# One selection product and a reciprocal of 512 columns in the second attention of a two-layer kernel

## The chip, the cores and the metric

The kernel runs on one core of a Trainium2 chip. The metric is the time of one execution on the device, in microseconds (us), lower being better. The engines are TensorE (PE in the profile; its weight loads are PEld), VectorE (DVE), ScalarE (ACT), GpSimd (POOL) and SyncE (SP, which here only issues transfers).

## The reference, cut to what matters

A batch of 8 sequences of 512 tokens with 256 channels goes through two layers, each an attention and a feed-forward part. The second attention, in which the change lies, has 16 heads of 16 channels, masked scores of 512 queries by 512 keys for each head, and a softmax:

```
scores = jnp.einsum('bhqd,bhkd->bhqk', query, key) / jnp.sqrt(jnp.asarray(D_K, query.dtype))
scores = jnp.where(m == 0, NEG_INF, scores)
probs = jax.nn.softmax(scores, axis=-1)
out = jnp.einsum('bhqk,bhkd->bhqd', probs, value)
out = out.transpose(0, 2, 1, 3).reshape(bs, -1, D_MODEL)
return out @ Wo + bo
```

The kernel divides by the softmax's sums only after the product with the values. The values carry a column of ones, so each head's result has 16 rows of channels and one row with the sum.

## The kernel before, in words

The kernel has three stages one after the other: `first_layer`, `cross_attention` (the second attention) and `experts` (the last feed-forward part). All that is said below is of `cross_attention`.

The 8 sequences are its batches. The 16 heads of a batch are taken in 4 groups of 4 heads, numbered through all batches as g = 0 to 31. A group takes 4 units, one for each 128 keys, so there are 128 units, and some more ahead and behind. Every engine has a program of its own that runs over the same units in order (`UNITS_RUN`), and semaphores tie the programs together. There is no planner: the order within a unit is written out in each engine's loop.

In one unit, for each of 4 heads (k = 0 to 3), TensorE makes the scores of 128 keys by 512 queries (`scores`: a bias product, line 1063, and the product of keys and queries, line 1064), and ScalarE takes their exponential (line 1202). Beside that, for each k, TensorE makes one product of 128 queries by 512 keys for a head of a group that comes 6 units later (`scores_for_maximum`, line 1049), and VectorE takes its masked row maximum (`maximum`, line 1321). These products have two banks, so TensorE waits before the third for VectorE to be through with the first (`wait(pe, s1_used, m - 1)`). Maxima end with unit 121.

After the four k, TensorE does in this order: the early events of bank `ps_m`, the product of the exponentials with the values of the unit before (`values`, line 1076), the query and key/value projections of a later token tile (once in 4 units each; for tiles up to 31), and the late events of bank `ps_m`. The maxima of a group are split in two parts (`split_maxima`, lines 1331 and 1333), turned by TensorE (event rows, line 1099), copied (line 1213) and placed as two more rows of the queries by a transfer (line 1220), for which the first scores of that group wait. Once in a batch, at the start of the batch's ninth unit, SyncE issues 24 transfers that spread the split queries and keys of the next batch (`spread_part`, line 872), after the rows of the group then due have landed.

The sums of group g are treated so:

- ScalarE copies the group's result to OT, 128 rows by 512 queries, head j in rows 32j to 32j+16 (`copy_o`, line 1208). The sum of head j is row 32j+16.
- Late in unit 4g+5 TensorE takes the sums out (event sums, line 1103): four products with OT as weights and the 4 columns of `pick`, so that the 512 queries lie on the partitions, 4 sums for each.
- At the end of unit 4g+5 VectorE inverts these 16 columns (`invert_sums`, line 1339) and copies each value 32 times (line 1341).
- Late in unit 4g+6 TensorE turns the result back with 4 transposes (event spread, line 1106), and VectorE multiplies OT by it (`divide`, line 1346).
- At the start of unit 4g+6 VectorE does the next `split_maxima` and then two maxima.

Of the kernel before, what the change touches and what calls it, by code (L numbers as in the profile page):

```python
# [11 lines left out]
P = 128  # L12
# [3 lines left out]
TPB = SEQ // P  # L16
# [713 lines left out]
def bank_m_events(unit):  # L730

    early, late = [], []
    if group_at(unit - 5) is not None:
        late.append(("sums", group_at(unit - 5)))
    if group_at(unit - 6) is not None:
        late.append(("spread", group_at(unit - 6)))
    if group_at(unit + 2) is not None:
        early.append(("rows", group_at(unit + 2)))
    b, u = divmod(unit, UNITS)
    if 1 <= b <= BATCH and u in (3, 4):  # L740
        early.append(("output", TPB * (b - 1) + 2 * (u - 3)))
        late.append(("output", TPB * (b - 1) + 2 * (u - 3) + 1))
    return early, late


def cross_attention(nc, ctxT, mask, maskT, L1, X, tg, ident_f, stats, mu_rs, kept, ahead):
# [3 lines left out]
    with ExitStack() as ctx:  # L750
# [14 lines left out]
        ident_b = sb("ident_b", [P, P], BF16)  # L765
        pick = sb("pick", [P, 4])
        v_scale, v_shift = sb("v_scale", [P, GROUPS]), sb("v_shift", [P, GROUPS])
# [14 lines left out]
        OT = sb("OT", [P, SEQ])  # L782
        r4 = sb("r4", [P, TPB, 4])
        r32 = sb("r32", [P, TPB, 4, 32])
        OTn = sb("OTn", [P, GROUPS, SEQ])
# [38 lines left out]
        for unit in UNITS_RUN:  # L824
            for events in bank_m_events(unit):
                for e in events:
                    m_use[e], m_before[e], last = len(m_use), last, e
                    if e[0] in ("spread", "output"):
                        m_freed[e] = len(m_freed) + 2
# [91 lines left out]
        def _(pool):  # L921
# [5 lines left out]
            def constants():  # L927
                pool.memset(ident_b[:, :], 0.0).then_inc(consts, 1)
                pool.memset(pick[:, :], 0.0).then_inc(consts, 1)
                pool.memset(v_scale[:, :], 0.0).then_inc(consts, 1)  # L930
                pool.memset(v_shift[:, :], 0.0).then_inc(consts, 1)
                pool.memset(wo[:, :, :], 0.0).then_inc(consts, 1)
                for p in range(3):
                    pool.memset(V[p][:, :, :, DH:VW], 1.0).then_inc(consts, 1)
                pool.wait_ge(consts, 4)
                pool.affine_select(out=ident_b[:, :], in_=ident_b[:, :], compare_op=ALU.not_equal, fill=1.0,
                                   base=0, pattern=[[-1, P]], channel_multiplier=1).then_inc(consts, 1)

                pool.affine_select(out=pick[:, :], in_=pick[:, :], compare_op=ALU.not_equal, fill=1.0,
                                   base=-DH, pattern=[[-32, 4]], channel_multiplier=1).then_inc(consts, 1)  # L940

# [67 lines left out]
        def _(pe):  # L1009
# [70 lines left out]
            def bank_m(event):  # L1080
                what, n = event
                if what == "rows":
                    pe.wait_ge(max_split, n + 1)
                elif what == "sums":
                    pe.wait_ge(o_sb, n + 1)
                elif what == "spread":
                    pe.wait_ge(inverted, n + 1)
                before = m_before[event]
                if before is None:
                    pe.wait_ge(m_free, 1)  # L1090
                elif before[0] == "rows":
                    pe.wait_ge(rows_sb, before[1] + 1)
                elif before[0] == "sums":
                    pe.wait_ge(inverted, before[1] + 1)
                else:
                    pe.wait_ge(m_free, m_freed[before])
# [4 lines left out]
                elif what == "sums":  # L1101
                    for q in range(TPB):
                        mm = pe.matmul(ps_m[:, 4 * q:4 * q + 4], OT[:, q * P:(q + 1) * P], pick[:, :], start=True, stop=True)
                elif what == "spread":
                    for q in range(TPB):
                        mm = pe.transpose(ps_m[:, q * P:(q + 1) * P], r32[:, q, :, :].rearrange("p j c -> p (j c)"), ident_f[:, :])
                else:
# [43 lines left out]
        def _(act):  # L1151
# [52 lines left out]
            def copy_o(g):  # L1204
                act.wait_ge(pv_done, TPB * (g + 1))
                if g:
                    act.wait_ge(m_free, m_freed["spread", g - 1])
                act.activation(OT[:, :], ps_o, ACT.Copy).then_inc(o_sb, 1)
# [43 lines left out]
        def _(dve):  # L1252
# [82 lines left out]

            def invert_sums(g):
                use = m_use["sums", g]
                dve.wait_ge(m_ready, use + 1)
                steps.done(dve.reciprocal(r4[:, :, :].rearrange("p q h -> p (q h)"), ps_m[:, 0:4 * TPB]))
                steps.wait()  # L1340
                dve.tensor_copy(r32[:, :, :, :], r4[:, :, :].unsqueeze(3).broadcast_to([P, TPB, 4, 32])).then_inc(inverted, 1)

            def divide(g):
                use = m_use["spread", g]
                dve.wait_ge(m_ready, use + 1)
                dve.tensor_tensor(OTn[:, g % GROUPS, :], OT[:, :], ps_m, ALU.mult).then_inc(m_free, 1)
# [13 lines left out]
            for unit in UNITS_RUN:  # L1360
# [19 lines left out]
                for what, n in late:  # L1380
                    if what == "sums":
                        invert_sums(n)
                    elif what == "spread":
                        divide(n)
# [615 lines left out]
```

## Time and profile before

| What | Before |
|---|---|
| median of 3 runs | 2315.28 us (2314.14 to 2317.16) |
| the profiled execution, its own time | 2316.27 us |
| its span, first to last instruction | 2314.5 us |
| TensorE busy, share of the span | 85% |
| VectorE busy, share of the span | 68% |
| mean granted TensorE clock | 0.914 |
| second attention, from about | 560 us to 1451 us |

Busy time of TensorE is the time in which at least one product runs, and a product's end is modelled, so two neighbours overlap in the records; the pitch from one start to the next tells what a product costs. A releaser is the instruction whose signal ended a wait.

### The profile page before, as it was taken

The page shows a single profiled execution, that of the slowest core. Times are in us where ns is not written, and L with a number is a line of the kernel's source. Part 1 is how long each engine was busy: PE and PEld are TensorE (multiplying, and loading weights), DVE is VectorE, ACT ScalarE, POOL GpSimd, SP SyncE. Part 2 cuts the span into 40 slices and gives each one's busy share as a digit, 9 for nine tenths or more (in the row PEclk, how much of TensorE's full clock was granted, in tenths as well). Part 3 has the DMA queues.
Part 4 walks back from the last instruction along what each step waited for, and adds up shares of the span by engine and source line. Part 5 has one row for each costly group of instructions (what it writes and reads, how often), then busy time and mean ns, then how long its engine had stood idle before and what let it go on. Part 6 is the DMA issues. An engine that isn't in the chain of part 4 may idle for free. (4 is left out here: it accounts for less than half of the span.)

```text
span 2314.5 us, 35806 instructions
## 1 busy us (share of the span) xinstructions
PE 1966.5 (85%) x12086; PEld 1392.0 (60%) x12086; DVE 1576.7 (68%) x3208; ACT 1059.8 (46%) x2039; POOL 919.2 (40%) x671
## 2 busy tenths in 40 slices
PE   5889888977598988989898989700999999999998
PEld 3566666664233433434343434600999999999998
DVE  7999999984565655656565753630777777777775
ACT  2233434433255554545555544210566566556554
POOL 6988888863433332323332200155222222222222
PEclk9899999988699999999999998555999999999999
DMA  7100000101624425151515310242566666666662
GB/s 286 43 10 8 10 10 10 35 1 34 109 74 67 84 53 102 32 105 33 97 60 78 76 21 1 73 173 91 189 222 227 211 225 222 224 224 216 228 216 68
DMA packets 146909, 245.79 MB, mean 106 GB/s; under 512 B 14235, under 2 KB 92143, under 8 KB 146802
## 3 DMA queue, kind: packets, MB, share of 16 engines
q1 hardware_dynamic: 135660, 218.93, 34.1%
q0 software_dynamic: 10624, 25.26, 2.9%
q8 instruction: 56, 0.92, 0.2%
q14 instruction: 51, 0.42, 0.1%
q10 hardware_dynamic: 518, 0.27, 0.0%
HBM read 201.96 MB, written 45.76 MB: 107 GB/s over the span
## 5 line engine op out<-in xcount | busy, mean ns | idle before, releaser
L1321 DVE CUSTOM_DVE_ANT_0 x_dump<-x_ps,x_bias_q 128x512 bf16<-128x512 f32 x512 | 353.3, 690 | 200.6 <-PE x_ps L1049 188.1
L1202 ACT ACTIVATE x_PT<-x_ps 128x512 f32<-128x512 f32 x512 | 290.1, 601 | 292.2 <-PE x_ps L1064 289.3
L1063 PE MATMUL x_ps<-x_bias_k,x_ident_b 128*128 128x512 bf16 x512 | 201.1, 393 | 66.5 <-DMA x_QS<-x_rows 66.4
L1852 ACT ACTIVATE e_silu<-m_ps 128x256 f32<-128x256 f32 x312 | 118.6, 380 | 231.9 <-PE m_ps L1789 231.9
L1756 POOL DMA_INDIRECT out_dram<-e_y,e_label x78 | 78.9, 1012 | 365.4 <-DVE e_y L1908 353.6
L1049 PE MATMUL x_ps<-x_KS,x_QS 96*128 96x512 bf16 x512 | 203.6, 399 | 12.0 <-DVE x_mx L1321 11.5
L1064 PE MATMUL x_ps<-x_QS,x_KS 98*128 98x512 bf16 x512 | 200.2, 391 | 0.0
L1891 DVE TENSOR_TENSOR e_gated<-e_silu,m_ps 128x256 f32<-128x256 f32 x312 | 120.7, 417 | 102.5 <-ACT e_silu L1852 98.0
L1789 PE MATMUL m_ps<-e_x_lo,m_hi 128*128 128x256 f32 x640 | 181.1, 283 | 1.5 <-DVE e_x_lo L1876 1.5
L1789 PE MATMUL m_ps<-e_x_hi,m_lo 128*128 128x256 f32 x640 | 181.0, 283 | 0.0
L1789 PE MATMUL m_ps<-e_x_hi,m_hi 128*128 128x256 f32 x640 | 180.7, 282 | 0.0
L1789 PE MATMUL m_ps<-e_x_hi,e_hi 128*128 128x256 f32 x608 | 171.1, 281 | 0.0
L1789 PE MATMUL m_ps<-e_x_lo,e_hi 128*128 128x256 f32 x608 | 171.1, 281 | 0.0
L1789 PE MATMUL m_ps<-e_x_hi,e_lo 128*128 128x256 f32 x608 | 171.1, 281 | 0.0
L1458 DVE TENSOR_TENSOR m_lo<-m_raw,m_hi 128x2048 fp32r<-128x2048 f32 x60 | 137.2, 2287 | 38.2 <-ACT m_hi L1454 38.2
L282 POOL TENSOR_TENSOR a_pool_pv<-a_e,a_v 128x2304 f32<-128x2304 f32 x32 | 162.6, 5080 | 0.0
L1749 POOL DMA_INDIRECT e_y<-out_dram,e_label x78 | 84.6, 1084 | 164.1 <-DMA out_dram<-e_y,e_label 137.7
L1458 DVE TENSOR_TENSOR e_lo<-m_raw,e_hi 128x2048 fp32r<-128x2048 f32 x57 | 130.4, 2287 | 26.3 <-ACT e_hi L1454 26.3
L1076 PE MATMUL x_ps<-x_PT,x_V 128*17 128x512 f32 x1024 | 136.9, 598 | 0.0
L1063 PEld LDWEIGHTS x_ps<-x_bias_k,x_ident_b 128*128 128x128 bf16 x512 | 53.8, 105 | 132.2 <-DMA x_QS<-x_rows 81.9
L1049 PEld LDWEIGHTS x_ps<-x_KS,x_QS 96*128 96x128 bf16 x512 | 50.9, 100 | 124.7 <-DVE x_mx L1321 91.7
L1454 ACT ACTIVATE m_hi<-m_raw 128x2048 fp32r<-128x2048 f32 x60 | 115.0, 1916 | 23.0 <-DMA m_raw<-in_L_ffn_w_dram 23.0
(291 smaller groups left out, 5517.4 us busy)
## 6 DMA issues: line engine op xcount, KB each, us to landing
m_raw<-in_L_ffn_w_dram SPq DMA_DIRECT2D x117, 1024.0 KB, 5.1
parts<-x_part SPq DMA_DIRECT2D x24, 512.0 KB, 3.7
expert_in<-a_blank SPq DMA_DIRECT2D x1, 10062.0 KB, 28.4
e_x<-expert_in SPq DMA_DIRECT2D x39, 258.0 KB, 5.8
x_QS<-parts SPq DMA_DIRECT2D x48, 192.0 KB, 8.8
x_KS<-parts SPq DMA_DIRECT2D x48, 192.0 KB, 12.1
next_mask_k<-in_maskT_dram SPq DMA_DIRECT2D x32, 256.0 KB, 2.7
next_mask_q<-in_mask_dram SPq DMA_DIRECT2D x29, 256.0 KB, 2.8
```

The lines of the kernel that those rows point to most:

```text
L282: pool.tensor_tensor(heads(pool_pv[:, :], PV_POOL), probabilities(e_[t % 2][:, PV_OWN * H:], PV_POOL), values(v_sb[t % 3][:, :], PV_POOL), ...
L1049: pe.matmul(ps_max[m % 2], QS[b % 2][0:HROWS, h, q * P:(q + 1) * P], KS[b % 2][0:HROWS, h, :], start=True, stop=True).then_inc(s1_ps, 1)
L1063: pe.matmul(ps_st[e % 3], ident_b[:, :], bias_k[b % 2][:, kc, :], start=True, stop=False)
L1064: pe.matmul(ps_st[e % 3], KS[b % 2][:, h, kc * P:(kc + 1) * P], QS[b % 2][:, h, :], start=False, stop=True).then_inc(st_ready, 1)
L1076: mm = pe.matmul(ps_o[32 * j:32 * j + VW, :], V[b % 3][:, kc, 4 * g + j, :], PT[unit % 2][:, j, :], start=(kc == 0), stop=(kc == TPB - 1))
L1202: act.activation(PT[unit % 2][:, k, :], ps_st[e % 3], ACT.Exp, scale=DH ** -0.5).then_inc(exp_done, 1)
L1321: dve.tensor_tensor_reduce(out=dump[:, :], in0=ps_max[m % 2], in1=bias_q[b % 2][:, q, :], scale=1.0, scalar=NEG, op0=ALU.add, op1=ALU.max, ...
L1454: act.activation(w_hi[p][n][:, :, :], raw[n][:, :, :], ACT.Copy).then_inc(hi_done[n], 1)
L1458: eng.tensor_tensor(w_lo[p][n][:, :, :], raw[n][:, :, :], w_hi[p][n][:, :, :].bitcast(F32), ALU.subtract)\
L1789: mm = pe.matmul(out, left[a], right[b], start=first and n == 0, stop=last and n == 2)
L1852: act.activation(silu[f % 2][:, :], ps_h[f % 4][:, 0:BLK], ACT.Silu).then_inc(silu_done, 1)
L1891: dve.tensor_tensor(gated[k % 2][:, n, :], silu[n][:, :], ps_h[f % 4][:, BLK:2 * BLK], ALU.mult)\
```

## The change

The transposes of the event spread go, and so do the tiles `r4` and `r32` and the function `invert_sums`. `pick` becomes 128 columns wide: column 32j+c has its one in row 32j+16, for each c of 0 to 31. It is now the weights, and OT streams: one product of 128x128 weights with 512 columns puts each head's sum in all 32 rows of that head. VectorE takes the reciprocal of the whole 128x512 bank in place, in `divide`, and multiplies OT by it right after; both are late in unit 4g+5. The wait of the next user of `ps_m`, and of the next `copy_o`, is for `divide` in that unit.

```diff
-    if group_at(unit - 6) is not None:
-        late.append(("spread", group_at(unit - 6)))
...
-        pick = sb("pick", [P, 4])
+        pick = sb("pick", [P, 4, 32])
...
-        r4 = sb("r4", [P, TPB, 4])
-        r32 = sb("r32", [P, TPB, 4, 32])
...
-                    if e[0] in ("spread", "output"):
+                    if e[0] in ("sums", "output"):
...
-                pool.memset(pick[:, :], 0.0).then_inc(consts, 1)
+                pool.memset(pick[:, :, :], 0.0).then_inc(consts, 1)
...
-                pool.affine_select(out=pick[:, :], in_=pick[:, :], compare_op=ALU.not_equal, fill=1.0,
-                                   base=-DH, pattern=[[-32, 4]], channel_multiplier=1).then_inc(consts, 1)
+                pool.affine_select(out=pick[:, :, :], in_=pick[:, :, :], compare_op=ALU.not_equal, fill=1.0,
+                                   base=-DH, pattern=[[-32, 4], [0, 32]], channel_multiplier=1).then_inc(consts, 1)
...
-                elif what == "spread":
-                    pe.wait_ge(inverted, n + 1)
...
-                elif before[0] == "sums":
-                    pe.wait_ge(inverted, before[1] + 1)
...
-                    for q in range(TPB):
-                        mm = pe.matmul(ps_m[:, 4 * q:4 * q + 4], OT[:, q * P:(q + 1) * P], pick[:, :], start=True, stop=True)
-                elif what == "spread":
-                    for q in range(TPB):
-                        mm = pe.transpose(ps_m[:, q * P:(q + 1) * P], r32[:, q, :, :].rearrange("p j c -> p (j c)"), ident_f[:, :])
+                    mm = pe.matmul(ps_m, pick[:, :, :].rearrange("p j c -> p (j c)"), OT[:, :], start=True, stop=True)
...
-                    act.wait_ge(m_free, m_freed["spread", g - 1])
+                    act.wait_ge(m_free, m_freed["sums", g - 1])
...
-            def invert_sums(g):
-                use = m_use["sums", g]
-                dve.wait_ge(m_ready, use + 1)
-                steps.done(dve.reciprocal(r4[:, :, :].rearrange("p q h -> p (q h)"), ps_m[:, 0:4 * TPB]))
-                steps.wait()
-                dve.tensor_copy(r32[:, :, :, :], r4[:, :, :].unsqueeze(3).broadcast_to([P, TPB, 4, 32])).then_inc(inverted, 1)
-
             def divide(g):
-                use = m_use["spread", g]
-                dve.wait_ge(m_ready, use + 1)
+                dve.wait_ge(m_ready, m_use["sums", g] + 1)
+                dve.reciprocal(ps_m, ps_m).then_inc(inverted, 1)
+                dve.wait_ge(inverted, g + 1)
                 dve.tensor_tensor(OTn[:, g % GROUPS, :], OT[:, :], ps_m, ALU.mult).then_inc(m_free, 1)
...
                     if what == "sums":
-                        invert_sums(n)
-                    elif what == "spread":
                         divide(n)
```

## Rows read from the trace of the kernel before

**Rows 1.** Windows, 1050 to 1100 us: time, busy (count) per engine, PEclk, DMA.
```profile
1050.00:1100.00 50.00, 49.51 (x259) 22.70 (x257) 32.14 (x103) 26.47 (x55) 15.28 (x16) 1.00 0.12 38
```

**Rows 2.** Waits, 700 to 1400 us: waiter, releaser, total us, times, longest.
```profile
PEld x_ps L1063 <- DMA x_QS<-x_rows: 77.2, 13, 12.3
PEld x_ps L1049 <- DVE x_mx L1321: 68.3, 190, 0.6
```

**Rows 3.** Timeline, the unit after a group's sums: start, us, engine, instruction, idle before.
```profile
1045.63 1.05 PE L1103 MATMUL x_ps<-x_pick,x_OT 128*128 128x4 f32 x8
...
1046.55 0.38 PE L1063 MATMUL x_ps<-x_bias_k,x_ident_b 128*128 128x512 bf16 x1
...
1047.08 0.25 DVE L1339 RECIPROCAL x_r<-x_ps 128x16 f32<-128x16 f32 x1
...
1047.36 0.43 DVE L1341 COPY x_r<-x_r 128x512 f32<-128x512 f32 x1
...
1048.06 0.69 DVE L1321 CUSTOM_DVE_ANT_0 x_dump<-x_ps,x_bias_q 128x512 bf16<-128x512 f32 x1
...
1048.81 0.10 PEld L1049 LDWEIGHTS x_ps<-x_KS,x_QS 96*128 96x128 bf16 x1 [0.37 <-DVE x_mx L1321]
```

**Rows 4.** Timeline, TensorE's 128x512 f32 products of a key/value tile.
```profile
1039.66 1.96 PE L1015 MATMUL x_ps<-next_wkv,next_cT 128*128 128x512 f32 x4 [0.32 <-ACT x_full L1184]
1041.55 0.39 PE L1017 MATMUL x_ps<-next_bias,x_ones 3*128 3x512 bf16 x1
```

**Rows 5.** Timeline, the end of another unit 4g+6.
```profile
1021.38 0.66 PE L1106 MATMUL x_ps<-ident_f,x_r 128*128 128x128 f32 x4
...
1021.88 0.38 PE L1063 MATMUL x_ps<-x_bias_k,x_ident_b 128*128 128x512 bf16 x1
...
1022.08 0.69 DVE L1346 TENSOR_TENSOR x_OTn<-x_OT,x_ps 128x512 f32<-128x512 f32 x1 [2.06 <-PE x_ps L1106]
```

**Rows 6.** Groups of instructions by form on VectorE: count, busy us, mean ns.
```profile
L1339 DVE RECIPROCAL x_r<-x_ps 128x16 f32<-128x16 f32 x32 | 8.1, 254 | 19.5 <-PE x_ps L1103 19.5
L555 DVE RECIPROCAL a_rden<-a_den 128x16 f32<-128x16 f32 x32 | 7.8, 243 | 0.0
L1647 DVE RECIPROCAL r_share<-r_den 128x32 f32<-128x32 f32 x1 | 0.4, 353 | 0.0
```

**Rows 7.** Timeline, SyncE's and ScalarE's transfers of one batch, and TensorE's wait.
```profile
1002.58 1.26 SPq L872 DMA_DIRECT2D x_QS<-parts  x3
...
1022.51 1.19 ACTq L1220 DMA_DIRECT2D x_QS<-x_rows  x2
...
1033.08 0.61 PE L1063 MATMUL x_ps<-x_bias_k,x_ident_b 128*128 128x512 bf16 x1 [7.38 <-DMA x_QS<-x_rows]
```

**Rows 8.** Windows of 4 us after waits of TensorE; PEclk is the last number but two.
```profile
716.20:720.20 4.00, 4.00 (x13) 2.03 (x14) 0.98 (x3) 1.19 (x2) 1.92 (x1) 0.54 0.24 67
...
1002.60:1006.60 4.00, 4.00 (x13) 2.03 (x14) 1.40 (x4) 1.28 (x3) 0.35 (x1) 0.57 0.39 110
...
1340.60:1344.60 4.00, 4.00 (x10) 1.45 (x11) 1.40 (x4) 1.61 (x3) 1.92 (x1) 0.51 0.02 8
...
1108.50:1112.50 4.00, 4.00 (x24) 1.67 (x24) 2.58 (x7) 3.00 (x8) 1.11 (x1) 1.00 0.43 110
```

**Rows 9.** Timeline of TensorE, two of the short waits for rows.
```profile
1002.58 0.39 PE L1063 MATMUL x_ps<-x_bias_k,x_ident_b 128*128 128x512 bf16 x1 [1.94 <-DMA x_QS<-x_rows]
...
1108.48 0.39 PE L1063 MATMUL x_ps<-x_bias_k,x_ident_b 128*128 128x512 bf16 x1 [1.18 <-DMA x_QS<-x_rows]
```

**Rows 10.** Timeline, groups without maxima: sums of group 29, and the last group.
```profile
1409.74 0.26 DVE L1339 RECIPROCAL x_r<-x_ps 128x16 f32<-128x16 f32 x1 [0.98 <-PE x_ps L1103]
...
1411.40 0.33 PE L1099 MATMUL x_ps<-x_ident_b,x_mp 128*8 128x128 bf16 x3
...
1431.80 0.26 DVE L1339 RECIPROCAL x_r<-x_ps 128x16 f32<-128x16 f32 x1 [4.73 <-PE x_ps L1103]
...
1433.34 0.69 DVE L1346 TENSOR_TENSOR x_OTn<-x_OT,x_ps 128x512 f32<-128x512 f32 x1 [0.81 <-PE x_ps L1106]
```

## The prediction

> **What bounds the kernel now.** I read the windows first, for the stage in which the change lies. In a stretch of 50 us in mid-stage TensorE is busy 49.51 us at full granted clock, VectorE 32.14 us [rows 1]. So TensorE sets the pace, and VectorE has a third of its time free. The list of waits says how near the two are. TensorE's weight load for the maximum products waited 190 times for VectorE, 68.3 us in all and never over 0.6 us [rows 2]: with two banks for these products, TensorE is held at once when VectorE falls behind. The only long waits of TensorE are those for rows placed by a transfer, 77.2 us in 13 waits, up to 12.3 us [rows 2]. So three questions decide: what TensorE saves, how long VectorE is away from the maxima in one piece, and which waits for rows are there to swallow that.
>
> **TensorE: the sums.** The four old products and their eight passes hold TensorE from 1045.63 to 1046.55, 0.92 us [rows 3]. The new one is a 128x512 product in f32. Two such products, four passes, took from 1039.66 to 1041.55, 1.89 us, so one costs 0.95 us [rows 4]. The step is worth nothing: 0.03 us a group, 1 us in all, left out of the sum.
>
> **TensorE: the transposes.** They hold TensorE from 1021.38 to 1021.88, 0.50 us, at the end of unit 4g+6 [rows 5]. Over 32 groups that is 16 us at most. It pays only where TensorE doesn't wait next for a transfer. Seven groups lie in front of the long wait for rows (below), and about six in front of a short one like those of 1.94 and 1.18 us [rows 9]; there the wait grows by what was saved. That leaves 19 x 0.50 = 9.5 us. The multiplication in the same place had VectorE wait 2.06 us for the transposes [rows 5]; that was idle time of an engine that wasn't late, and its going gives nothing.
>
> **VectorE: one long piece.** Before, the work between the sums and the next `split_maxima` is the reciprocal at 1047.08 and the copy that ends at 1047.79, 0.71 us; after it come the split, and at 1048.06 the first maximum of unit 4g+6 [rows 3]. TensorE's third maximum product of that unit, at 1048.81, waits for this maximum (0.37 us idle of the weight load) [rows 3]. So this one maximum is on the path already: each microsecond that VectorE adds ahead of it reaches TensorE whole. The change puts here a reciprocal of 512 columns and the multiplication, 0.69 us [rows 5], with about 0.06 us between them for the semaphore (1047.33 to 1047.36 between the two old steps [rows 3], rounded up).
>
> The trace has no reciprocal of 512 columns. It has 16 columns in 243 ns from SBUF and 254 ns from PSUM, and 32 columns in 353 ns [rows 6]. The two from SBUF give (353 - 243)/16 = 6.9 ns a column, and 243 - 16 x 6.9 = 133 ns fixed. For 512 columns: 0.133 + 512 x 0.0069 = 3.65 us. Bounds: 0.69 us below, if the two short ones were all fixed cost and a column cost what it does in the multiplication of the same 128x512 shape [rows 5]; above, 353/32 = 11 ns a column in proportion, 5.65 us. I take 3.65, since two lengths of the same operation give it; the 32-column row is a single one, and an error of 20 ns in it moves the slope by 1.25 ns and the result by 0.6 us, so 3.1 to 4.3 is its own spread.
>
> The Trainium skill bears on this price. "VectorE: DVE Perf Modes", in "First, the fixed hardware budget", says that reciprocal is an iterated division with a repeat count of 8, and gives VectorE 0.96 GHz. As an estimate from that page, 8 cycles a column would be 8.3 ns, 4.27 us for 512 columns with no fixed part. The rows give 6.9 ns, a little less, and no run here yet shows which holds at this length; the sum goes by the rows, and the longer one is a rival.
>
> New piece: 3.65 + 0.06 + 0.69 = 4.40 us; less 0.71 is 3.7 us later for the first maximum, and so for TensorE. In that time TensorE does three heads' scores and two maximum products and then stands still for some 3.5 us. Behind it in its queue are the rest of the maxima products, the values, the rows of a later group and the projections, and ScalarE's exponentials wait for those. Nothing makes it good later, since TensorE has no free time.
>
> **How often it is paid.** Maxima end with unit 121, so 29 groups (g = 0 to 28) have them in unit 4g+6. Once a batch SyncE's 24 spreading transfers start (1002.58); the rows that ScalarE issues at 1022.51 lie behind them and land only at 1033.08, after TensorE has waited 7.38 us [rows 7]. The four units between hold one late unit 4g+5 and its follower. A TensorE that is 3.7 us later there only waits less, since the transfers' 30.5 us don't depend on it. This wait is there in all seven batches that have a successor. So 29 - 7 = 22 groups pay: 22 x 3.7 = 81.4 us.
>
> Groups without maxima: for g = 29 the next thing on TensorE that needs VectorE is the turning of rows at 1411.40 [rows 10]. Sums came at 1409.74; 4.40 us of division and 0.35 us of splitting put that product at about 1414.4, +3.0 us. For g = 30 only the 0.50 us is gained, counted above. For the last group nothing covers: before, reciprocal at 1431.80 to the end of the multiplication at 1434.03, 2.23 us [rows 10]; after, 4.40 us, +2.2 us. Together 5.2 us. The wider `pick` is made once on GpSimd in start-up; its cost (a fraction of a microsecond against 4 columns) I leave out.
>
> **The clock.** The same stalls touch TensorE's clock. After the long waits of 7.4 to 11.4 us the next 4 us are granted 0.50 to 0.61, seven times of seven (the first and the last shown), and after a wait of only 1.94 us they are granted 0.57 [rows 8, 9], against the full clock before. After waits of 1.2 us and less it stayed at 1.00, four of four (one shown) [rows 8, 9]. A stall of 3.5 us is nearer to the first kind. Some 4 us at the level of 1.2 GHz instead of 2.4 do half the work, 2 us lost at most. As part of the low stretch can fall into the stall itself, I take 1.5 us a stall, between 0 and 2.0. For 22 groups and g = 29: 23 x 1.5 = 34.5 us.
>
> **Sum.** -9.5 + 81.4 + 5.2 + 34.5 = 111.6 us. The span of 2314.5 becomes 2426. The profiled execution took 2316.27, 1.8 us more than its span, and 1.0 us more than the median of 2315.28; from the median the sum gives 2427 us.
>
> **The rivals.**
> - *The clock holds.* The stalls come one a group, with about 20 us of dense work between; the 1.94 us wait is one case only. Then 2427 - 34.5 = 2392 us.
> - *A longer reciprocal*, 4.4 us: +0.75 on 22 groups, g = 29 and the last is +18, 2445 us. For it: the one row of 32 columns may be short of the true slope. (This is about what the Trainium skill's repeat count would give.)
> - *A short reciprocal*, near the 0.69 us of the multiplication: the maximum comes 0.69 + 0.06 + 0.69 - 0.71 = 0.73 us later, too short for the clock by the waits of 1.2 us. 22 x 0.73 - 9.5 + 1 = +8, 2323 us. Against it: 32 columns cost 110 ns more than 16 [rows 6], where 16 columns at the multiplication's rate would be about 20 ns.
> - *Faster: the division fits into VectorE's free time.* VectorE's third of free time [rows 1] would have to lie ahead of the first maximum of unit 4g+6. The gain would be the transposes' 9.5 us alone, 2306 us. The place is the first maximum after the sums, the price the reciprocal: with 22 x (r + 0.06 + 0.69 - 0.71) = 9.5 it decides below r = 0.39 us. Against it: 16 columns alone cost 0.25 us, and even the plain copy of 512 columns 0.43 us [rows 3].
>
> That the change doesn't do what it says can't well be: the transposes are gone from the program.
>
> **How the numbers follow.** Chances: forecast 0.48, clock holds 0.20, longer reciprocal 0.22, short reciprocal 0.06, faster 0.04. The time is that of the first, 2427 us. The first three hold 0.90; their own bounds run from 2380 (clock at full, reciprocal 3.1 us: 2392 - 0.55 x 24 = 2379) to 2460 (2445 and 23 x 0.5 more clock loss give 2457), which leaves out the last two and the far end of each. A measurement of this kernel can tell about 0.2% (4.6 us) from no change. Of the short reciprocal's 0.06 about half would fall within that: faster 0.04, same 0.03, slower 0.93.
>
> **What would show it.** Right: a reciprocal of 128x512 of 3.1 to 4.4 us, 32 times; TensorE waiting for a maximum of VectorE at line 1049's successor some 3.5 us once in four units; the long waits for rows down by some 4 us each; no transposes from the turned sums; low pieces in the granted clock after the stalls. Wrong: if the reciprocal is right and the loss per group is under 3 us, something makes good what TensorE lost; if the clock row stays at 1.00 in windows after stalls, the 34.5 us fall away; if the seven long waits don't shrink, 7 x 3.7 = 26 us come on top.

## The result, and the profile after

| | before | after |
|---|---|---|
| median of 6 runs each | 2316.22 us (2314.14 to 2321.21) | 2421.65 us (2415.19 to 2427.43) |
| profiled execution / its span | 2316.27 / 2314.5 us | 2417.3 / 2415.6 us |
| mean granted TensorE clock | 0.914 | 0.898 |

The ratio is 1.045, with a 95% interval of 1.043 to 1.0471: 105 us slower. The forecast was 2427 us.

The page of the kernel after, its first part and the granted clock in 40 slices:

```profile
span 2415.6 us, 35038 instructions
...
PE 1996.7 (83%) x11702; PEld 1371.1 (57%) x11766; DVE 1661.8 (69%) x3176; ACT 1065.8 (44%) x2039; POOL 918.3 (38%) x671
...
PEclk9899999987799899989889889855799999999999
```

Windows (time, busy and count by engine, granted clock, DMA share, GB/s): first the stage's main part before, then the kernel after:

```profile
660.00:1430.00 770.00, 695.98 (x3616) 293.31 (x3614) 453.01 (x1429) 401.95 (x808) 201.55 (x200) 0.96 0.35 65
```

```profile
1050.00:1100.00 50.00, 39.71 (x164) 13.54 (x165) 30.03 (x81) 21.37 (x43) 13.21 (x14) 0.83 0.49 68
660.00:1430.00 770.00, 642.28 (x2825) 246.30 (x2877) 474.81 (x1267) 359.58 (x723) 201.48 (x200) 0.90 0.34 65
1091.40:1095.40 4.00, 3.94 (x17) 1.03 (x18) 2.10 (x6) 1.18 (x2) 0.00 (x0) 0.57 0.33 98
```

TensorE was busy for all of the 50 us before [rows 1]; now it is idle for ten of them, and the clock that it is granted is 0.83 there instead of 1.00. VectorE's busy time in that window is *not* larger (30.0 against 32.1 us), though it is over the whole stretch from 660 to 1430 us (474.8 against 453.0). Neither number says whether the amount of its work or the place of it holds TensorE up; the experiments with extra reciprocals below do. The list of waits names the holder (waiter, releaser, total us, times, longest), 700 to 1400 us:

```profile
PEld x_ps L1045 <- DVE x_mx L1309: 138.7, 164, 3.9
PE x_ps L1045 <- DVE x_mx L1309: 78.8, 27, 3.4
...
PEld x_ps L1059 <- DMA x_QS<-x_rows: 33.9, 12, 5.7
```

The line 1049 of before is 1045 now, and 1321 is 1309. The weight load's wait for the maximum has doubled and its longest is 3.9 us, where none was over 0.6 [rows 2]. The wait for the placed rows has shrunk from 77.2 to 33.9 us: that is where part of the delay went. The same place in time order (start, us, engine, instruction, idle before), answering to [rows 3]:

```profile
1084.91 1.12 PE L1094 MATMUL x_ps<-x_OT,x_pick 128*128 128x512 f32 x2
...
1085.87 0.38 PE L1059 MATMUL x_ps<-x_bias_k,x_ident_b 128*128 128x512 bf16 x1
...
1086.35 3.36 DVE L1326 RECIPROCAL x_ps<-x_ps 128x512 f32<-128x512 f32 x1
...
1087.84 0.38 PE L1060 MATMUL x_ps<-x_QS,x_KS 98*128 98x512 bf16 x1
...
1089.75 0.69 DVE L1328 TENSOR_TENSOR x_OTn<-x_OT,x_ps 128x512 f32<-128x512 f32 x1
1090.35 0.17 DVE L1319 TENSOR_SCALAR x_mp<-x_mx 128x16 bf16<-128x16 f32 x1
1090.55 0.18 DVE L1321 SCALAR_TENSOR_TENSOR x_mp<-x_mx,x_mp 128x16 bf16<-128x16 f32 x1
1090.70 0.69 DVE L1309 CUSTOM_DVE_ANT_0 x_dump<-x_ps,x_bias_q 128x512 bf16<-128x512 f32 x1
...
1091.46 0.40 PE L1045 MATMUL x_ps<-x_KS,x_QS 96*128 96x512 bf16 x1 [3.24 <-DVE x_mx L1309]
...
1092.07 0.63 PE L1060 MATMUL x_ps<-x_QS,x_KS 98*128 98x512 bf16 x1
```

The new product holds TensorE 0.96 us (1084.91 to 1085.87). The reciprocal takes 3.36 us; then come multiplication, split and the first maximum, and only then can TensorE go on, after 3.24 us of standing still. The last row shows the second loss: a product that took 0.38 us takes 0.63, and the window from 1091.40 is granted 0.57.

The transfers of one batch, which answer to [rows 7], and the division without cover in the last group, to [rows 10]:

```profile
1040.50 1.26 SPq L868 DMA_DIRECT2D x_QS<-parts  x3
...
1065.29 1.20 ACTq L1208 DMA_DIRECT2D x_QS<-x_rows  x2
...
1071.77 0.61 PE L1059 MATMUL x_ps<-x_bias_k,x_ident_b 128*128 128x512 bf16 x1 [3.30 <-DMA x_QS<-x_rows]
...
1534.92 3.37 DVE L1326 RECIPROCAL x_ps<-x_ps 128x512 f32<-128x512 f32 x1 [4.23 <-PE x_ps L1094]
1538.32 0.69 DVE L1328 TENSOR_TENSOR x_OTn<-x_OT,x_ps 128x512 f32<-128x512 f32 x1
```

From the first of SyncE's transfers to the product that the rows release are 31.3 us (30.5 before), so a later TensorE only waits less: 3.30 us where it was 7.38. The seven long waits were 8.38, 8.49, 8.60, 7.38, 7.47, 8.46 and 11.42 us before, and are 4.79, 3.64, 4.57, 3.30, 3.11, 4.72 and 7.32 now.

**A ruler for the rest.** I measure from one group's sums product to the next in the trace and average over the first 24 groups by their place in a batch: A from the first group to the second, B to the third, C to the fourth, D to the first of the next batch. B holds the long wait for rows; early in A lay some of the short waits. "All" sums the 24 intervals and the 7 after them, in us:

| kernel | A | B | C | D | first 24 | last 7 | all |
|---|---|---|---|---|---|---|---|
| before | 22.80 | 31.70 | 21.43 | 28.86 | 628.7 | 127.9 | 756.6 |
| after | 25.53 | 32.49 | 26.21 | 33.68 | 707.4 | 152.5 | 859.9 |
| no_reciprocal | 22.60 | 31.69 | 20.92 | 28.34 | 621.3 | 125.6 | 746.9 |
| filler | 24.32 | 32.01 | 24.38 | 31.75 | 674.8 | 142.8 | 817.6 |
| in_slack | 22.64 | 31.71 | 22.46 | 29.81 | 639.7 | 138.9 | 778.6 |
| in_two | 22.77 | 31.62 | 21.54 | 29.82 | 634.5 | 133.4 | 767.9 |
| late_invert | 22.75 | 31.88 | 21.95 | 29.38 | 635.7 | 129.3 | 765.0 |
| extra_in_place | 26.47 | 32.61 | 26.30 | 33.84 | 715.3 | 129.1 | 844.4 |

All of the difference between the two profiles lies there: the groups took 103.3 us more, what is ahead of them 0.2 less, what is behind them 2.0 less, of 101.1 us between the spans.

### The profile page after: what moved, and what is told of

It reads as the page before. It is cut to its first block and busy times, and to the rows that moved or that the text cites. A ratio compares the mean times of both kernels' runs of the same rounds, so it can differ in the third digit from the quotient of the medians.

```text
span 2415.6 us, 35038 instructions
## 1 busy us (share of the span) xinstructions
PE 1996.7 (83%) x11702; PEld 1371.1 (57%) x11766; DVE 1661.8 (69%) x3176; ACT 1065.8 (44%) x2039; POOL 918.3 (38%) x671
## 5 line engine op out<-in xcount | busy, mean ns | idle before, releaser
L1045 PE MATMUL x_ps<-x_KS,x_QS 96*128 96x512 bf16 x512 | 212.2, 416 | 107.5 <-DVE x_mx L1309 107.2
L1060 PE MATMUL x_ps<-x_QS,x_KS 98*128 98x512 bf16 x512 | 206.5, 403 | 14.0 <-DMA x_QS<-x_rows 7.7
L1059 PE MATMUL x_ps<-x_bias_k,x_ident_b 128*128 128x512 bf16 x448 | 181.7, 406 | 23.8 <-DMA x_QS<-x_rows 23.8
L1072 PE MATMUL x_ps<-x_PT,x_V 128*17 128x512 f32 x1024 | 159.9, 681 | 0.0
L1326 DVE RECIPROCAL x_ps<-x_ps 128x512 f32<-128x512 f32 x32 | 107.6, 3363 | 23.1 <-PE x_ps L1094 23.1
```

Source lines behind the costliest of these rows:

```text
L1045: pe.matmul(ps_max[m % 2], QS[b % 2][0:HROWS, h, q * P:(q + 1) * P], KS[b % 2][0:HROWS, h, :], start=True, stop=True).then_inc(s1_ps, 1)
L1059: pe.matmul(ps_st[e % 3], ident_b[:, :], bias_k[b % 2][:, kc, :], start=True, stop=False)
L1060: pe.matmul(ps_st[e % 3], KS[b % 2][:, h, kc * P:(kc + 1) * P], QS[b % 2][:, h, :], start=False, stop=True).then_inc(st_ready, 1)
L1072: mm = pe.matmul(ps_o[32 * j:32 * j + VW, :], V[b % 3][:, kc, 4 * g + j, :], PT[unit % 2][:, j, :], start=(kc == 0), stop=(kc == TPB - 1))
```

## The experiments

Ratios are to the kernel before, measured beside each run, with their 95% intervals.

**no_reciprocal.** What is the rest of the change worth? The kernel after without its division, so that VectorE multiplies by the sums themselves:

```diff
-                dve.reciprocal(ps_m, ps_m).then_inc(inverted, 1)
-                dve.wait_ge(inverted, g + 1)
```

> The changed kernel without its reciprocal: VectorE multiplies by the sums themselves in the same place, so the division is left out and nothing else. Theory of the stall (one long piece of VectorE work ahead of the first maximum after the sums holds TensorE, and the stall also costs clock): the piece shrinks from 3.36 + 0.69 us to 0.69 us, about what stood there before the change (0.71), so the stalls of 3.24 us and the low clock after them go, and the transposes' 0.50 us stay saved in some 19 groups: 2300 to 2312 us, about 2305. Rival (TensorE's new product or the earlier release of the bank is what costs): at least 2400 us.

2298.91 us, ratio 0.9926 (0.9908 to 0.9944), 1 us below what was expected. The sums product stands here as in the kernel after, and the stalls are gone; the groups took 9.7 us less than before, for the 9.5 of the forecast. The spans differ by 14.7 us. The other 5.0 us lie outside the groups: 2.4 us more ahead of them and 7.4 us less behind the last one. That last part took 876 us here, 884 before and 879 to 885 in the other profiles; some 1.5 us of it can be the last group's missing inversion, and the rest I don't credit to the edit. So everything that the change costs is the reciprocal's, and inside the groups it could bring about 10 us at best.

**half_reciprocal and quarter_reciprocal.** Does the loss follow the reciprocal's length? The kernel after with the reciprocal of 256 or 128 of the 512 columns, the rest left undivided (the half's edit is shown):

```diff
-                dve.reciprocal(ps_m, ps_m).then_inc(inverted, 1)
+                dve.reciprocal(ps_m[:, 0:256], ps_m[:, 0:256]).then_inc(inverted, 1)
```

> The changed kernel with the reciprocal of the first 256 of 512 columns only; the division of the other half is left out. Stall theory: the reciprocal takes about 1.75 us, the first maximum comes 1.8 us later than before the change, the stall of TensorE is about 1.6 us in 29 groups and 22 pay: 2348 us if the clock holds after a stall of 1.6 us, up to 2380 if it falls every time; I expect about 2365 and see in the trace after how many stalls the clock fell. Rival (the loss is in proportion to VectorE's added work and nothing else): half of 105 us, 2369 us, with no low clock at all or low clock in proportion.

> The changed kernel with the reciprocal of the first 128 of 512 columns only; the division of the rest is left out. By the lengths measured so far (1.76 us for 256 columns, 3.36 for 512) it takes 0.96 us, and the first maximum comes 0.96 + 0.06 + 0.69 - 0.71 = 1.0 us later than before the change, so TensorE stands still about 0.9 us. Stall and clock theory: after so short a stall the clock holds, as it did 25 times of 25 after 1.26 us, and only the stall is paid: 2316 + 22 x 1.0 - 9.5 = 2329 us, 2320 to 2336; the step from 128 to 256 columns (about 45 us) is then much larger than in proportion, because it brings the low clock. Rival (the loss is proportional to the columns, the clock is a by-product): a quarter of the way from 2299 to 2422 and on the line through 2375 at 256 columns, 2337 us or more.

Half: 2375.2 us, 1.0258 (1.024 to 1.0277). Quarter: 2352.21 us, 1.0164 (1.0143 to 1.0186), 23 us above what was expected: a miss. The groups of instructions on VectorE (count, busy us, mean ns), of the kernel after and of the quarter:

```profile
L1326 DVE RECIPROCAL x_ps<-x_ps 128x512 f32<-128x512 f32 x32 | 107.6, 3363 | 23.1 <-PE x_ps L1094 23.1
```

```profile
L1326 DVE RECIPROCAL x_ps<-x_ps 128x128 f32<-128x128 f32 x32 | 30.8, 962 | 24.0 <-PE x_ps L1094 24.0
...
L1321 DVE SCALAR_TENSOR_TENSOR x_mp<-x_mx,x_mp 128x16 bf16<-128x16 f32 x32 | 29.0, 905 | 1.1
```

With 1762 ns for 256 columns, the reciprocal costs (3363 - 962)/384 = 6.25 ns a column and 0.16 us beside. The second row shows the miss: a step of the split that took 0.18 us takes 0.91 on average. In time order, in the quarter kernel:

```profile
1067.24 0.96 DVE L1326 RECIPROCAL x_ps<-x_ps 128x128 f32<-128x128 f32 x1
...
1068.97 1.15 POOL L969 TENSOR_TENSOR x_part<-x_rest,x_part 128x512 bf16<-128x512 f32 x1 [2.14 <-ACT x_part L1183]
1069.04 1.11 DVE L1321 SCALAR_TENSOR_TENSOR x_mp<-x_mx,x_mp 128x16 bf16<-128x16 f32 x1
...
1070.82 0.39 PE L1045 MATMUL x_ps<-x_KS,x_QS 96*128 96x512 bf16 x1 [1.72 <-DVE x_mx L1309]
```

The step begins 0.07 us after an instruction of GpSimd's and ends at 1070.15, within 0.03 us of that one's end at 1070.12. So the stall is 1.7 us and not 0.9. In the half kernel the other step of the split took 0.52 us instead of 0.17, beside the same instruction of GpSimd's, and its stall was 2.0 us, not 1.6:

```profile
1076.04 1.16 POOL L969 TENSOR_TENSOR x_part<-x_rest,x_part 128x512 bf16<-128x512 f32 x1 [2.14 <-ACT x_part L1183]
1076.10 0.69 DVE L1328 TENSOR_TENSOR x_OTn<-x_OT,x_ps 128x512 f32<-128x512 f32 x1
1076.71 0.52 DVE L1319 TENSOR_SCALAR x_mp<-x_mx 128x16 bf16<-128x16 f32 x1
```

In the full kernel the split falls elsewhere and keeps its 0.17 and 0.18 us. The last groups, where GpSimd has no such instruction, serve as a check within the same kernels. In the quarter kernel the step took 1.01 to 1.11 us in all 25 groups in which it met the instruction and 0.18 us in the five behind them; in four of these TensorE still had a maximum to wait for, and stood 1.0 to 1.1 us, near the 0.9 that was expected. In the half kernel the step went from 0.52 back to 0.17 us there. The multiplication at 1076.10 above, which reads one of its inputs from PSUM, kept its 0.69 us beside the same instruction.

The Trainium skill, "SBUF — State Buffer", section "SBUF: two separate sides", says that GpSimd and a VectorE operation with two inputs from SBUF share ports by an exclusive lock, and whoever comes second stands until the other's whole instruction is over. The quarter kernel's step has two such inputs, and its end agrees with that to within 0.15 us: 0.18 us of work after GpSimd's end at 1070.12 would end at 1070.30, and it ended at 1070.15. The half kernel's step has one input; the page names one-input operations only in a mode that uses two ports, and no run shows whether this one was in it. That the two instructions must meet is shown; that it is this lock stays argued.

The time of the quarter kernel alone would fit the rival of its expectation, 2337 us or more. But the loss is not in proportion to the columns. Over no_reciprocal the intervals between the groups' sums (the ruler) grew by 52.0, 70.3 and 113.0 us for 128, 256 and 512 columns, while the stalls were 1.7, 2.0 and 3.2 us: the loss follows the stall.

**extra_in_place, extra_elsewhere, elsewhere_clean.** Is it VectorE's load, or its place? The kernel *before*, with a 512-column reciprocal of unused data added at the end of a unit, 24, 24 and 18 times:

```diff
+                if unit % 4 == 1 and 4 < unit < 101:
+                    dve.wait_ge(s1_used, 4 * (unit + 7))
+                    with nc.allow_low_precision(reason="scratch"):
+                        steps.done(dve.reciprocal(dump[:, :], wo[:, 0:2, :].rearrange("p g n -> p (g n)")))
+                    steps.wait()
```

This is extra_in_place, at the end of units 4g+5. Extra_elsewhere has the condition `unit % 4 == 0 and 3 < unit < 100`, the end of units 4g+4; elsewhere_clean leaves out units 16b+4 besides.

> The kernel before with all its work, and 24 more reciprocals of 128x512 from and to SBUF, whose result nobody reads, right behind the inversion at the end of units 4g+5 for g = 0 to 23. Stall theory: it is the same piece in the same place as in the changed kernel; 6 of the 24 lie in front of the long wait for rows, 18 pay 3.4 us and about 1.7 us of clock: 2316 + 92 = 2408 us, 2390 to 2420. Rival that it is the release of the bank or the new product that costs: 2316 us.

> The same 24 extra reciprocals as in the other kernel of this pair, but at the end of units 4g+4, in which TensorE has a key/value projection of 1.9 us after the last maximum product, and VectorE had some 3.6 us free in the trace of the kernel before. Stall theory: they fit, no stall over 0.3 us, the clock holds: 2316 us, 2312 to 2322. Rival (the amount of VectorE work decides): as much as the kernel with the same reciprocals in the other place, about 2408 us.

> The kernel before with 18 extra reciprocals of 128x512 at the end of units 4g+4, as in the run with 24, but none in the units in which VectorE takes an output late (there five pieces began only in the next unit and stalled TensorE for 3.2 us each). Stall theory: VectorE's free time holds all 18, 60 us of added VectorE work cost nothing: 2314 us, 2308 to 2320. Rival (amount of VectorE work): 18 x 3.4 us, 2375 us.

| run | median us | ratio |
|---|---|---|
| extra_in_place | 2401.28 | 1.0382 (1.036 to 1.0403) |
| extra_elsewhere | 2340.83 | 1.0113 (1.0088 to 1.0137) |
| elsewhere_clean | 2315.93 | 0.9997 (0.9985 to 1.0009) |

The same instruction costs 3.7 us each in the one place (by the ruler 88 us for 24, with the slower clock's part included) and, within the interval of 0.12%, nothing in the other (60 us of VectorE's time in 18). In place each of 24 left TensorE standing for 3.25 to 3.33 us. Elsewhere went over its expectation, and the trace says why: 19 were free, but 5 of the 6 in units 16b+4 came behind an output that VectorE takes late there, and so slid into the next unit. One of the five:

```profile
1001.26 0.48 DVE L1351 SCALAR_TENSOR_TENSOR X<-x_ps,tanh_g,X 128x256 f32<-128x256 f32 x1 [3.80 <-PE x_ps L1111]
...
1002.12 3.33 DVE L1390 RECIPROCAL x_dump<-x_wo 128x512 bf16<-128x512 f32 x1
...
1006.25 0.61 PE L1049 MATMUL x_ps<-x_KS,x_QS 96*128 96x512 bf16 x1 [3.18 <-DVE x_mx L1321]
```

And a free one, from the clean kernel; no maximum product of TensorE's is due until 1063.36, and the weight load behind it waits 0.34 us, as ever:

```profile
1060.44 3.35 DVE L1390 RECIPROCAL x_dump<-x_wo 128x512 bf16<-128x512 f32 x1
...
1063.36 0.38 PE L1049 MATMUL x_ps<-x_KS,x_QS 96*128 96x512 bf16 x1
...
1063.91 0.69 DVE L1321 CUSTOM_DVE_ANT_0 x_dump<-x_ps,x_bias_q 128x512 bf16<-128x512 f32 x1
...
1064.67 0.10 PEld L1049 LDWEIGHTS x_ps<-x_KS,x_QS 96*128 96x128 bf16 x1 [0.34 <-DVE x_mx L1321]
```

**filler.** How much is the clock's? The kernel after with 20 products of unused data in the stall of 22 of the 29 groups, in a free half bank:

```diff
+                    if k == 2 and unit % 4 == 2 and unit % UNITS != 10 and 4 < unit < 120:
+                        for n in tiles_at(unit - 2):
+                            pe.wait_ge(xT_sb, n + 1)
+                        for _ in range(20):
+                            pe.matmul(ps_p[:, D:2 * D], ident_b[:, :], bias_k[unit // UNITS % 2][:, 0, 0:D], start=True, stop=True)
```

> The changed kernel, all its work unchanged, with 20 products of 128x256 bf16 more on TensorE in the stall of 3.24 us of each group (not in the groups that lie in front of the long wait for rows), written to a free half bank and read by nobody. They take some 2.2 to 2.6 us at full clock, so they end before VectorE's first maximum and cost no time of their own, but TensorE is no longer idle for over a microsecond. Theory that the stall costs clock as well: the clock stays at full level after most stalls, and the time falls by up to the 35 us that I put down to it: 2422 - 30 = 2392 us, 2380 to 2400. Rival (the whole loss is the stall itself, and the low clock costs nothing, since VectorE sets the pace there): 2422 us or a little more.

2379.63 us, 1.0277 (1.0255 to 1.0298): more work on the engine that bounds the kernel, and 42 us less than without it.

```profile
1073.62 2.36 PE L1120 MATMUL x_ps<-x_bias_k,x_ident_b 128*128 128x256 bf16 x20 [0.60 <-ACT x_xn L1147]
...
1076.26 0.39 PE L1045 MATMUL x_ps<-x_KS,x_QS 96*128 96x512 bf16 x1 [0.28 <-DVE x_mx L1314]
```

and windows of 12 us round a stall, of this kernel and of the one after:

```profile
1070.00:1082.00 12.00, 11.08 (x64) 5.16 (x62) 9.43 (x19) 5.38 (x11) 3.76 (x4) 1.00 0.10 34
```

```profile
1084.00:1096.00 12.00, 8.73 (x40) 2.85 (x40) 9.32 (x22) 4.82 (x10) 4.23 (x5) 0.86 0.11 33
```

The maximum comes no earlier (the real product still waits for it, 0.28 us behind the filling), but the granted clock is 1.00 where it was 0.86. The clock fell after none of the 22 filled stalls and after all 7 that were left open. By the ruler, intervals C and D are 1.8 and 1.9 us shorter than in the kernel after, and A, where the clock had held after two of the six stalls, 1.2.

**in_slack and in_two.** Can the same division be placed where VectorE is free? ScalarE copies the sums to SBUF (0.61 us), which frees the bank, and VectorE divides after the last maximum of unit 4g+6; in_two does 384 columns there and 128 and the multiplication one unit later (all at once for the last group of a batch):

```diff
+            def copy_sums(g):
+                act.wait_ge(m_ready, m_use["sums", g] + 1)
+                wait(act, divided, g)
+                act.activation(sums_sb[:, :], ps_m, ACT.Copy).then_inc(m_free, 1)
...
                     maximum(m)
+                if group_at(unit - 6) is not None:
+                    divide(group_at(unit - 6))
                 for what, n in late:
-                    if what == "sums":
-                        divide(n)
```

> The same new product, the same reciprocal of 512 columns and the same multiplication as in the changed kernel, but ScalarE first copies the sums to SBUF (0.6 us of its free time), and VectorE divides after the last maximum of unit 4g+6 instead of ahead of the first. In the trace of the kernel before, VectorE was free there for some 2.9 us before TensorE could need it. Stall theory: a piece of 4.1 us leaves a stall of about 1.2 us, the invert's 0.7 us is gone from the place that was on the path, and the clock holds mostly: about 2330 us, 2310 to 2345. Rival (the amount of VectorE work decides, wherever it stands): no change from the changed kernel, about 2420 us.

> The new product, with ScalarE copying the sums to SBUF, and VectorE's reciprocal cut in two: 384 columns at the end of unit 4g+6, 128 columns and the multiplication at the end of unit 4g+7 (both at the end of 4g+6 for a batch's last group, whose output is due). Stall theory: in groups 0 and 2 of a batch nothing stalls and the transposes' 0.50 us are saved; the last group of each batch still pays 1.0 us, and the groups after the last token tile (24 on), where units are short, pay 1 to 2 us each: 2312 to 2326 us, about 2320. A time under 2306 would beat both kernels. Rival: no better than with the division in one piece, 2341 us.

In_slack: 2341.11 us, 1.0098 (1.0068 to 1.0127). In_two: 2325.86 us, 1.0048 (1.0028 to 1.0068). One place in in_slack:

```profile
1057.68 3.35 DVE L1335 RECIPROCAL x_sums_sb<-x_sums_sb 128x512 f32<-128x512 f32 x1
...
1061.06 0.69 DVE L1337 TENSOR_TENSOR x_OTn<-x_OT,x_sums_sb 128x512 f32<-128x512 f32 x1
...
1062.42 0.39 PE L1046 MATMUL x_ps<-x_KS,x_QS 96*128 96x512 bf16 x1 [1.26 <-DVE x_mx L1318]
```

The same 4 us of VectorE's work stall TensorE for 1.26 us instead of 3.24, and the clock fell after none of these 24 stalls. In the last groups, where no projections of a next tile keep TensorE busy, the stall was 2.6 us, and the clock fell after 4 of 5. Cutting the piece in two brings interval C to 21.54 us, 0.1 above before. Both times lie at the upper end of what was expected. Both took back most of the 105 us, neither got below before.

**late_invert.** Was the 0.37 us idle of the weight load [rows 3] a loss that a later inversion would win back? The kernel before, the small reciprocal and the copy moved behind the second maximum of unit 4g+6:

```diff
+                if group_at(unit - 6) is not None:
+                    invert_sums(group_at(unit - 6))
...
-                    if what == "sums":
-                        invert_sums(n)
```

> The kernel before with one move: the short inversion (0.71 us on VectorE) comes after the second maximum of unit 4g+6 instead of ahead of the first; all work stays. Stall theory: the first maximum after the sums was on the path already before the change, so TensorE's third and fourth maximum products of that unit come 0.35 to 0.45 us earlier in the 22 groups that pay: about 2307 us, 2303 to 2312. Rival (the 0.37 us of idle weight load there was no loss for TensorE, and only longer pieces count): 2316 us, the same as before.

2323.21 us, 1.0032 (1.0019 to 1.0046): a miss, slower instead of faster.

```profile
1075.34 1.15 POOL L973 TENSOR_TENSOR x_part<-x_rest,x_part 128x512 bf16<-128x512 f32 x1 [2.13 <-ACT x_part L1195]
...
1076.09 0.69 DVE L1341 COPY x_r<-x_r 128x512 f32<-128x512 f32 x1
...
1076.92 0.33 PE L1099 MATMUL x_ps<-x_ident_b,x_mp 128*8 128x128 bf16 x3 [0.58 <-DVE x_r L1341]
```

The third maximum product came 2.24 us after its unit's start against 2.27 before, and the fourth 2.89 against 3.00: a gain of 0.11 us at most, and not 0.35 to 0.45. Idle time of the weight load is not lost time of TensorE: it loads ahead, beside the product that runs. In the new place the copy runs beside GpSimd and takes 0.69 us instead of 0.43, and TensorE's next user of the bank, the turning of rows, waits for it: 0.52 us in each of C and D.

**act_log.** ScalarE in VectorE's place, with exp(-ln(sum)):

```diff
+                act.activation(sums_sb[:, :], ps_m, ACT.Ln).then_inc(m_free, 1)
...
+                act.activation(sums_sb[:, :], sums_sb[:, :], ACT.Exp, scale=-1.0).then_inc(inverted, 1)
```

> The new product as in the changed kernel, but ScalarE makes the reciprocal as exp(-ln(sum)), in two passes of about 0.6 us in unit 4g+6, and VectorE only multiplies, after the last maximum of that unit. The stall on VectorE is gone and the 0.50 us of the transposes stay saved, some 9.5 us: 2307 us if ScalarE's two passes lie in its free time. Against that, ScalarE's first pass stands between two exponentials and can hold the values by up to 0.6 us in 22 groups: 2320 us. If each change between logarithm and exponential loads a table (1.28 us where the trace of the kernel before has one), ScalarE is held 2.6 us more in each group: 2360 us or more. I expect 2312, 2300 to 2325.

2354.82 us, 1.0189 (1.0161 to 1.0216), 43 us over what was expected. ScalarE's groups:

```profile
L1203 ACT ACT_TABLE_LOAD x32 | 41.1, 1283 | 0.6
L1193 ACT ACT_TABLE_LOAD x31 | 39.8, 1283 | 0.6
```

and the wait for the bank with the sums:

```profile
PE x_ps L1094 <- ACT x_sums_sb L1203: 44.4, 27, 1.7
```

Each logarithm loads a table, and the next exponential loads the old one again, 1.28 us each. In all there are 64 such loads, two for each of the 32 groups. The first holds the logarithm, and the product that wants its bank waits 1.7 us.

## Why the prediction was right, step by step

The mechanism was right: one long piece ahead of the first maximum after the sums, TensorE standing for its length, and the slower clock behind. That the time came within 6 us was in part luck: the stalls were forecast 13.7 us too high and the clock 7.8 us too low. In us, the groups' terms by the ruler:

| step | forecast | measured | from |
|---|---|---|---|
| new sums product | 0 | 0.96 against 0.92 a group | timeline |
| transposes | -9.5 | -9.7 | no_reciprocal less before |
| stalls, without the clock (81.4 and g = 29) | 84.4 | 70.7 | filler less no_reciprocal |
| clock | 34.5 | 42.3 | after less filler |
| sum in the groups | 109.4 | 103.3 | after less before |
| last group's tail | 2.2 | 1.9 (reciprocal to the end of the multiplication: 4.09 against 2.23) | timelines |

- **The length of the reciprocal.** Forecast 3.65 us, measured 3.36: 6.25 ns a column, where the two short rows gave 6.9. The repeat count of 8 that the Trainium skill names ("VectorE: DVE Perf Modes", "First, the fixed hardware budget") gave 4.27 us as an estimate; the measured 3.36 us doesn't bear that price out. The price of a stall was then 3.36 + 0.04 + 0.69 - 0.71 = 3.38 us and not 3.7; intervals C and D of filler less no_reciprocal give 3.46 and 3.41.
- **The first group of a batch.** I let the short waits take up the transposes' gain, and not the stall. That is inconsistent, and is the step that was wrong: where a wait would have swallowed 0.5 us of lead it also swallows delay. Interval A grew by 1.72 us only (filler less no_reciprocal), 1.7 less than C. The short waits at those places, of the kind of [rows 9], were 1.3 to 1.9 us in the six first groups of no_reciprocal, 1.6 us on average, and are gone from filler and from the kernel after: they took up what A didn't pay. As I read SyncE's queue, the rows that they waited for lie behind its transfers of a tile's parts, which the stall doesn't move; that is argued from the order of the queue alone. The forecast's 84.4 us were in the first 24 groups 66.6, measured 53.5: the price explains 18 x 0.32 = 5.8, interval A 6 x 1.7 = 10.0, and interval B gives 6 x 0.32 = 1.9 back. In the last seven 17.8 was forecast and 17.2 measured.
- **The last group.** Its tail grew by 1.9 us, but all that lies behind the groups took 2.0 us less in the profile, within the spread of that part, so the total doesn't test this term.
- **The long waits.** As forecast: all seven shrank, by 3.6 to 4.9 us, and interval B grew by 0.32 us without the clock.
- **"On the path already".** True in effect, and for the wrong reason. I took 0.37 us of the weight load's idle time as proof that TensorE was waiting. Late_invert shows that moving work away brings the next two maximum products only 0.03 and 0.11 us forward: maximum and TensorE were ready at nearly the same time, which is the point where any delay counts in full. It is extra_in_place, not the idle time of [rows 3], that shows this for delays.
- **The clock.** Low windows after the stalls, as forecast: the clock fell after 27 of 29. The price was too low: I took 1.5 us a stall, for a low stretch that falls in part into the stall. It was 1.8 and 1.9 in C and D, where all were followed by a fall, near the 2 us that I held for the most.
- **The rivals.** The clock did not hold, the reciprocal was neither longer nor short, and the division met a piece of VectorE's free time too late to use it. That free time exists, though: one unit earlier in elsewhere_clean, partly a few maxima later in in_slack. The "faster" rival failed on the place alone.

What stays open: by what mechanism GpSimd's instruction lengthens VectorE's short ones, what sets whether the clock falls after a stall (it held after two of 29 of the same length), and the 1 us or so left in the sum above.

## What to carry to other kernels

Where two engines hand two banks back and forth, an engine that is a third idle can still not take one long instruction: ask for the longest piece that fits between two hand-overs at that place, not for the share of free time. Test a delay's price by adding the same instruction to the old kernel, there and elsewhere: in place 3.7 us each, one unit earlier nothing. If a wait for a transfer hides a gain, it hides a loss too, up to its own length; book both or neither. A stall of TensorE can cost its length and then the slower clock behind it, here 1.8 to 1.9 us on 3.4.

## What the runs showed of the hardware

- **Granted clock after stalls.** It fell after 27 of 29 stalls of 3.23 to 3.48 us (the kernel after), all 24 of 3.25 to 3.33 us (extra_in_place) and 3 of 5 of 3.2 us (extra_elsewhere), after 24 of 29 of 1.8 to 2.1 us (half_reciprocal), 16 of 25 of 1.7 to 1.8 us (quarter_reciprocal), and none of 24 of 1.26 us (in_slack). But in act_log, in another place of the stage, it fell after only 2 of 24 gaps of 1.73 us: length alone doesn't tell. Useless products in the stall kept it at 1.00 and were worth 42 us.
- **VectorE beside GpSimd.** 128x16 steps went from 0.17 and 0.18 us to 0.52 and 1.11, and a 128x512 copy from 0.43 to 0.69, when a 1.15 us operation of GpSimd's ran beside them; a 128x512 multiplication with one input from PSUM kept its 0.69 us. A *shorter* reciprocal moved the split into that overlap, so that a quarter of the columns left half of the stall (1.7 of 3.2 us).
- **Reciprocal.** On 128 partitions in f32 it took 0.96, 1.76 and 3.36 us for 128, 256 and 512 columns, where a multiplication of 512 columns took 0.69 us.
- **Tables.** A logarithm among exponentials cost two loads of 1.28 us each time.
